# Four-layer transformer kernel: the first attention's output projection moved ahead of the scores and its two masks put together, and the rotary pad rows written once

## What is computed

```python
q = (x @ Wq).reshape(B, N, 16, 64).transpose(0, 2, 1, 3)
kv = x @ Wkv
s = einsum('bhid,bhjd->bhij', q * 64 ** -0.5, k)
gm = max(s, axis=-1, keepdims=True)
p = where(causal_mask, 0.0, exp(s - gm))
out = einsum('bhij,bhjd->bhid', p, v) / (sum(p, axis=-1, keepdims=True) + 1e-8)
return out.transpose(0, 2, 1, 3).reshape(B, N, 1024) @ Wo + bo
```

## Time and profile before

| | us |
|---|---|
| median of 3 runs | 2650.59 |
| lowest and highest | 2645.61, 2651.19 |
| the profiled execution's own time | 2643.31 |
| its span, first to last instruction | 2641.5 |
| first attention, first to last score product's start (L842) | 25.0 to 626.0 |
| first rotary phase's first DVE instruction | 1750.90 |
| second rotary phase's first DVE instruction | 2191.45 |
| mean granted TensorE clock (1 is full speed) | 0.972 |

### The profile page before, as it was taken

The page is one execution under the profiler, slowest core; times in us unless marked ns, Lnnn a source line. Parts: engine busy times, 40 slices in busy tenths (PEclk is TensorE's granted clock), DMA queues, the critical chain, the costliest instruction groups (busy, mean ns, idle before and its releaser), DMA issues. The chain is left out here.

```text
span 2641.5 us, 61743 instructions
## 1 busy us (share of the span) xinstructions
PE 2472.0 (94%) x19594; PEld 2043.2 (77%) x19656; DVE 1886.0 (71%) x5964; ACT 1462.7 (55%) x4040; POOL 644.7 (24%) x1166
## 2 busy tenths in 40 slices
PE   7999999998999999999998999978999687999899
PEld 6788888887888789999997888856666375666676
DVE  6777777776677478888887766756776345677698
ACT  6788888787444355666665333324555443455544
POOL 0000000001111100000101011127776035777422
PEclk8999999999999899999999999989999897999999
DMA  3200000002000345555554000037553735555100
GB/s 125 34 1 1 0 0 1 1 1 65 4 1 1 97 156 160 168 168 169 170 169 131 12 2 0 1 101 211 154 149 101 218 100 142 157 150 150 50 15 18
DMA packets 196813, 221.53 MB, mean 84 GB/s; under 512 B 12901, under 2 KB 180213, under 8 KB 195077
## 3 DMA queue, kind: packets, MB, share of 16 engines
q1 hardware_dynamic: 196612, 219.11, 28.5%
HBM read 118.42 MB, written 100.12 MB: 83 GB/s over the span
## 5 line engine op out<-in xcount | busy, mean ns | idle before, releaser
L907 DVE TENSOR_REDUCE a_nmax<-bank 128x2 f32<-128x512 f32 x256 | 165.0, 686 | 147.9 <-PE bank L842 147.7
L1481 ACT ACTIVATE a_p<-a_p,a_nmax 128x256 f32<-128x256 f32 x256 | 128.3, 502 | 198.2 <-DVE a_nmax L1682 194.5
L317 POOL TENSOR_TENSOR delta<-y,arena 128x256 f32<-128x256 f32 x30 | 23.2, 772 | 834.7 <-ACT y L310 834.7
L2194 ACT ACTIVATE a_p<-bank 128x1024 f32<-128x1024 f32 (+1 forms) x256 | 193.4, 808 | 21.5 <-PE bank L2255 17.2
L1785 ACT ACTIVATE f_silu<-bank 128x512 f32<-128x512 f32 x128 | 76.6, 599 | 204.6 <-PE bank L153 204.0
L2134 POOL TENSOR_SCALAR_AFFINE_SELECT a_p<-a_p 128x512 f32<-128x512 f32 x256 | 162.8, 636 | 0.0
L2413 DVE TENSOR_REDUCE a_nmax<-bank 128x4 f32<-128x1024 f32 x128 | 155.5, 1215 | 4.2 <-PE bank L2242 4.1
L1162 ACT ACTIVATE f_hidden<-bank,arena 128x512 f32<-128x512 f32 x128 | 87.6, 685 | 127.2 <-PE bank L153 127.2
L1236 PEld LDWEIGHTS bank<-arena,f_hidden 128*128 128x128 f32 x1024 | 135.4, 193 | 21.8 <-ACT f_hidden L1162 3.7
L1236 PE MATMUL bank<-arena,f_hidden 128*128 128x128 f32 x1024 | 144.8, 281 | 5.8 <-DVE f_acc L1303 1.8
L750 ACT CAST a_qk<-bank 128x256 fp32r<-128x256 f32 x256 | 95.1, 371 | 88.7 <-PE bank L153 88.6
(11 more groups left out here) (377 smaller groups left out, 7728.2 us busy)
## 6 DMA issues: line engine op xcount, KB each, us to landing
pos_dram<-a_pos SPq DMA_DIRECT2D x128, 383.0 KB, 2.8
a_stack<-rows_dram SPq DMA_DIRECT2D x128, 320.0 KB, 4.1
rows_dram<-a_cut SPq DMA_DIRECT2D x192, 192.0 KB, 2.5
a_shifted<-pos_dram SPq DMA_DIRECT2D x128, 256.0 KB, 2.6
merged_dram<-f_staged SPq DMA_DIRECT2D x16, 578.0 KB, 4.6
f_merged<-merged_dram SPq DMA_DIRECT2D x16, 578.0 KB, 6.3
gate<-gates_dram SPq DMA_DIRECT2D x32, 256.0 KB, 11.2
arena<-in_task SPq DMA_DIRECT2D x4, 1156.0 KB, 7.9
```

Source lines behind the costliest of these rows:

```text
L907: dve.tensor_reduce(nmax[:, at.ring(2), h, :], s_ps[h][:].rearrange("p (t k) -> p t k", t=NT), AX_X, ALU.max, negate=True).then_inc(s["nma ...
L1481: i = act.activation(p[:, at.ring(4), t, :], p[:, at.ring(4), t, :], ACT.Exp, bias=nmax[:, r, t:t + 1], accum_out=sums[:, r, t:t + 1])
L2194: act.activation(p[:, b4.ring(2), first:end], sT_ps[:, first:end], ACT.Exp).then_inc(s["exp"], 1)
```

## The change

In the first attention PE's output projection of step at-3 goes from the end of the step to a place between the transposes of p and the scores, with its waits for `oT` and, once a sequence, for `taken`; mask 1 goes from behind the value product to directly behind mask 0. The lists of ACT and DVE in that phase stay as they are. The pad rows of the rotary phases are set in the prologue and written by SP behind the gate loads of the first attention, into one DRAM tensor that both rotary phases then use; their own setting, writing and waiting go. The ones beside slot 0 of v are set at the very start of DVE's list, those of slots 1 to 3 where all four were, and ACT waits for them separately.

```diff
--- before.py
+++ after.py
@@ class Opening, __init__
+        self.pad = ctx.enter_context(nc.sbuf_tensor("open_pad", [ROPE_PADS, 2, T], BF16))
+        self.pad_set = ctx.enter_context(nc.semaphore("pad_set"))
@@ prologue, vector
+                dve.memset(opening.pad[:], 0.0).then_inc(opening.pad_set, 1)
+                dve.wait_ge(opening.pad_set, 1)
+                dve.memset(opening.pad[0:ROPE_SHIFTS, 1], 1.0).then_inc(opening.pad_set, 1)
                 mods(0, 0, 2)
@@ attention0, sync
                 load_gate(sp, k, phase)
                 load_gate(sp, k, phase + 1)
+                sp.wait_ge(opening.pad_set, 2)
+                for x in range(2):
+                    for which in range(2):
+                        rows = opening.pad[:, which]
+                        sp.dma_start(k.rows_dram[x, which, ROPE_ROWS:],
+                                     bass.AP(rows.tensor, rows.offset, [list(rows.ap[0]), [0, ROPE_HEADS], [1, T]])
+                                     ).then_inc(s["pads_out"], 16)
+                sp.wait_ge(s["pads_out"], 64)
@@ attention0, tensor
                             causal_transposes(pe, pT_ps[h], p[:, b2.ring(4), h, :], k.ident[:]).then_inc(s["pT_mm"], 1)
+                    if b3.real:
+                        wait(pe, s["oT"], b3)
+                        if b3.p == 0:
+                            wait(pe, s["taken"], b3.shift(-PER), item=True)
+                        for t in range(NT):
+                            mm = pe.matmul(y_ps[:, t * P:(t + 1) * P], oT[:, b3.ring(2), t * P:(t + 1) * P],
+                                           w["wo0"][:, b3.p, :], start=(b3.p == 0 and t == 0),
+                                           stop=(b3.p == LAST), skip_group_check=True)
+                        mm.then_inc(s["y_mm"], 1)
                     if at.real:
                         wait(pe, s["qk"], at, 2)
                         wait(pe, s["exp"], at.shift(-1), 2)
...
                     if at.real:
                         mask(0)
+                        mask(1)
                     if b2.real:
                         wait(pe, s["pT0"], b2)
...
                         mm.then_inc(s["o_mm"], 1)
-                    if at.real:
-                        mask(1)
-                    if b3.real:
...
-                        mm.then_inc(s["y_mm"], 1)
@@ build
+        k.rows_dram = nc.dram_tensor("rows_dram", (2, 2, ROPE_ROWS + ROPE_PADS, ROPE_HEADS, T), BF16, kind="Internal").ap()
@@ rope_attention
+ROPE_ROWS, ROPE_PADS, ROPE_SHIFTS, ROPE_HEADS = 72, 8, 2, 16
...
-        pad = sb("pad", [DH, 2, T], BF16)
...
-        rows_dram = nc.dram_tensor(f"rows_dram{phase}", (2, 2, PADDED, H, T), BF16, kind="Internal").ap()
+        rows_dram = k.rows_dram
@@ rope_attention, sync
-                sp.wait_ge(s["pad_set"], 2)
-                for x in range(2):
-                    for which in range(2):
...
-                                     ).then_inc(s["pad_in"], 16)
-                sp.wait_ge(s["pad_in"], 64)
@@ rope_attention, scalar
-                            if isinstance(at.base, int) and at.base == 0 and at.s == 1 - PER:
-                                act.wait_ge(s["ones"], 1)
+                            if isinstance(at.base, int) and at.base == 0 and at.s <= 1:
+                                act.wait_ge(s["ones"], 1 if at.s < 0 else 2)
@@ rope_attention, vector
-                dve.memset(pad[:], 0.0).then_inc(s["pad_set"], 1)
-                dve.wait_ge(s["pad_set"], 1)
-                dve.memset(pad[0:SHIFTS, 1], 1.0).then_inc(s["pad_set"], 1)
...
-                def ones_beside_values():
+                def ones_beside_values(slots):
-                    for x in range(4):
+                    for x in slots:
...
+                ones_beside_values((0,))
...
-                        ones_beside_values()
+                        ones_beside_values((1, 2, 3))
```

More of the change, by code:

```diff
@@ L697, in attention0 @@
         ht_ps = k.psum.rearrange("p (b c) -> p b c", b=8)[:, 4:6, C:512]
-        names = NORMS + ("xn", "ht_mm", "ht", "ht_rounded", "ht_cut", "gate_sign", "gate_size", "gates", "gates_out",
+        names = NORMS + ("xn", "ht_mm", "ht", "ht_rounded", "ht_cut", "gate_sign", "gate_size", "gates", "gates_out", "pads_out",
                  "qk_mm", "qk_rounded", "qk", "v_mm", "v", "s_mm",
@@ L1959, in _ @@
                 walk(dve, PER, 2, LEAD, LAG, step, PAIRS)
+ROPE_ROWS, ROPE_PADS, ROPE_SHIFTS, ROPE_HEADS = 72, 8, 2, 16
 def rope_attention(nc, d, k, phase):
     PER, H, DH, PARTS, G = 4, 16, 8, 3, 4
-    ROWS = DH * PARTS * PARTS
-    SHIFTS = 2
-    PADDED = ROWS + DH
+    ROWS, PADDED, SHIFTS = ROPE_ROWS, ROPE_ROWS + ROPE_PADS, ROPE_SHIFTS
     VP = 144 * G
@@ L1997, in rope_attention @@
                  "written_q", "written_k", "v_mm", "v", "s_mm", "nmax", "shift_hi", "shift", "shiftT_mm", "shiftT",
-                 "sT_mm", "exp", "causal", "spare", "o_mm", "o", "back_mm", "rec", "on", "oT_mm", "oT", "y_mm", "blank", "ones", "pad_set",
-                 "pad_in")
+                 "sT_mm", "exp", "causal", "spare", "o_mm", "o", "back_mm", "rec", "on", "oT_mm", "oT", "y_mm", "blank", "ones")
         s = signals(nc, ctx, f"a{phase}_", names + tuple(f"{x}{a}{b}" for x in ("stacked", "shifted")
@@ L2084, in write @@
                                      ).then_inc(written[which], 16)
-                sp.wait_ge(s["pad_set"], 2)
-                for x in range(2):
-                    for which in range(2):
-                        rows = pad[:, which]
-                        sp.dma_start(rows_dram[x, which, ROWS:PADDED],
-                                     bass.AP(rows.tensor, rows.offset, [list(rows.ap[0]), [0, H], [1, T]])
-                                     ).then_inc(s["pad_in"], 16)
-                sp.wait_ge(s["pad_in"], 64)
                 def step(at):
```

## The result

The changed kernel takes 2752.34 us (median of 4 runs, 2749.30 to 2755.95) where the kernel before took 2650.89 beside it. The ratio is 1.0371, with an interval from 1.0351 to 1.039: 101.5 us slower. The forecast was 2736, in a range from 2713 to 2770.

A forecast was written before the change was run, and what follows sets the result against it. Bound: in the first attention, a ring through TensorE and ScalarE (scores, projections, mask 0, exps, scores). Terms 95 + 2 - 2 - 5 = +90 on the profiled 2643.3 us: 2733, plus half the 7.3 offset: 2736 us, range 2713 to 2770.

The forecast's parts named there:

- The step: One step of the first attention's loop: 4.58 us plus 0.76 makes 5.34; over 125 steps +95 us.
- The handover behind the copy: From ScalarE's oT copy to TensorE's output projection in the first attention: 0.15 us, left the same.
- The take: Step in eight where ScalarE takes the previous sum: +0.54 us, 0.43 given back in the step behind; net +2 us.
- The masks: Mask 1 beside mask 0, first attention: cost 0 under VectorE's scaling, 37 us if that cover were gone; gain 0.
- the ring: Chain said to set the first attention's 4.58 us step: scores, projections, mask 0, exps of both heads, next scores.
- Lap ends: Five ScalarE stalls of about 1.6 us ahead of its pT copies: 0.4 of each absorbed, -2 us.
- Rotary: Openings of both rotary phases: first scores come sooner without the pads, 2.5 us each, -5 us; bounds 0 and -7.
- TensorE's stream as the bound: Rival, first attention: TensorE's queue sets the step, which shrinks by at most 0.12; 2627 us; chance 0.03, shared with queue reordering.
- The clock: Rival: TensorE falls from 2.4 to 1.2 GHz by stopping each step; four slow stretches +36, 2772 us; chance 0.07.
- Only the wait is paid: Rival, first attention: scores pay the wait for oT, the product is hidden; +33 - 5, 2675 us; chance 0.02.
- The step is dearer: Rival, first attention: drained product and no relief from GpSimd; +115 + 8 - 5, 2765 us with offset; chance 0.08.
- an idle ahead of the transposes: Sign of a wrong forecast: TensorE standing idle before the transposes in a first attention step; no size given.

## Why the prediction was right, and where its terms were off

**The mechanism held.** The scores wait for the copy of oT and then for four matmuls; the exps and the copy of oT end in the step where they ended. The output projection alone costs 0.81 a step. Two experiments that take away the wait, by different edits, both leave 0.37, so the wait is 0.44 and the place behind the transposes 0.37. The 0.44 are 0.33 of standing idle (the product starts at 4.75, and at 4.42 without the wait) and 0.10 by which the product that waited is longer. With the product ahead of the transposes as well, 0.10 is left; the masks alone cost as much, with TensorE's work in nearly the same order.

**The step: 5.34 forecast, 5.39 measured.** Two terms were mis-sized and partly cancel, which is luck. The handover behind the copy was "left the same" at 0.15; it is 0.06 (4.69 to 4.75), so that the wait came to 0.17 and not 0.26, below the bound of 0.19. The product was taken at 0.50, its start-to-start of before; it is 0.64. Of these 0.14, 0.10 come with the waiting: the same product in the same place takes 0.54 where it doesn't wait. That the start-to-start of a product that doesn't wait can't be carried over to one that does is the lesson of the term; my upper bound of 0.66 was named for the drain, and the 0.54 in front of the same scores speaks against that. Together +0.05, and 6 us over the steps.

The four fp32 matmuls at 128 columns took 0.54 without a wait, 0.135 each. The Trainium skill (TensorE: Matmul & The Clock Gate, "Back-to-back issue gap") gives about 81 ns; no row of this product comes near it, as the earlier trace rows had it already. The Trainium skill (TensorE: Matmul & The Clock Gate, "Architectural detail: the array is 16× 32×32, not 1× 128×128") says that TensorE's queue can pull weight loads ahead of matmuls in flight. The trace agrees behind the transposes where nothing is waited for, by 0.11 us, and shows a lead of at most 0.03 where the product waits, be it for oT or for the take.

**The take: +0.54 forecast, +0.60 and +0.55 measured**, in alternate sequences, and the 0.46 and 0.40 of the step behind it given back whole: +0.15 x 15, the 2 us of the forecast. The Trainium skill (SBUF — State Buffer, "SBUF: two separate sides") calls the port pair an exclusive lock, and the overlaps agree with it: the scaling took 1.01 us alone, 1.44 and 1.45 where it met one of GpSimd's operations, 1.77 where it met two. The longest single instruction of the scaling was 0.35 in the changed kernel, where it met none, and 0.74 in the one with the take moved, beside an operation of GpSimd's of 0.73.

**The masks: 0 forecast, 0 measured**, and for the reason given: mask 1 goes at 2.37 and the value product at 2.58 (2.4 and 2.6 forecast), under the cover of VectorE's scaling. But the prediction's price without the cover, 0.3 x 125, was too high; without it (masks alone) the step lost 0.10, because TensorE's queue had 0.12 of room behind the ring (transposes to scores 0.87 before, 0.75 there) and mask 1 gave back its 0.12 in the middle, while the product took 0.04 more.

**Lap ends: -2 forecast.** At one lap's end the pair of steps took 9.80 us before (5.13 and 4.67), 0.64 more than two regular ones, and 10.97 after, 0.19 more than two regular ones: 0.45 absorbed. Over the five it is 0.28 to 0.56, 2 us in all.

**Rotary: 2.3 to 2.5 a phase forecast, 2.2 (first) and 2.4 (second) measured**, by the path given. The second phase's first scores come 20.1 us after the feed-forward's last output product before and 17.7 after.

**The sum.** In the trace the first attention's 101.0 us are 0.81 in the 125 steps that hold the moved product, 101; 2 for the take; -2 for the lap ends; all other steps cancel out to within 1, by some luck: single steps at the start and the end differ by up to 1.9 either way. I had 95 for it. The medians differ by 101.5, and I had 90: with the 6 us of the first attention named, 5 are left, which is the reach of the ratio's interval. The other 4 us of the miss are the offset: I added half of the 7.3 us by which the profiled execution lay under the median, and the whole would have been right.

**The rivals.** TensorE's stream as the bound: no, it would have needed a copy of oT that ends ahead of the transposes. The clock: 1.00 between 220 and 300 us, and in every stretch from 92 to 668, in spite of a stop in each step; the 0.72 at the end of the phase stands over two of its 128 steps. "Only the wait is paid": no, the place costs 0.37. "The step is dearer" had the right sign for the product and the wrong reason, and GpSimd's relief came. One of my signs of a wrong forecast, an idle ahead of the transposes, did appear (0.29, released by "issue"); it costs nothing, since the copy of oT ends after them.

## What to carry to other kernels

Moving work across the instruction that closes a loop's ring was priced here by what it waits for (0.17) plus its full length (0.64), whatever TensorE's busy share said; and where the two chains were within 0.12 us of each other, each of the orders tried cost something. When a wait is moved, list what is queued behind it in the one step in eight as well as in the others: the take cost 1.98 us where the regular step cost 0.10. A group of matmuls that has to wait takes longer than one that doesn't, 0.10 us here, and its first weight load has lost its lead, whatever the wait is for.

## What the runs showed of the hardware that I had not expected

The handover from ScalarE's copy of oT to TensorE's first matmul took 0.04 to 0.06 us by the records, the one from its last accumulator read 0.15. It isn't a matter of the kind of instruction: the take, a copy too, was handed over in 0.05 in every second sequence and in 0.14 in the others. Why is open.

The second attention, whose code none of these kernels touches, took 500.7 us (first to last start of VectorE's addition at L1688, L1701 in the changed kernel) in the profiled execution of the kernel before, 513.0 in that of the changed kernel, and between 503.6 and 514.4 in those of the experiments. A part is the clock at its end: between 1520 and 1530 us of the changed kernel the granted clock was 0.72, and 41 matmuls ran, where the 10 us before and after have 73 and 71; in the kernel before it was 1.00 throughout. Most of the rest lies in the first 48 of the 128 steps (199.2 us against 191.0), and why is open. The 12.3 us are about what the two profiled executions, 112.6 us apart, differ more than the medians with their 101.5, and a reader who compares two traces from end to end has to take such a phase out first.
